# Start-up lookup of edges, PE's skip branches and the last norm in a four-layer graph network

## The reference

```python
# layer 0: out = segment_sum((x @ W)[src] * (edge_attr @ edge_w), dst) + b
# layer 1: agg = segment_sum(x[src], dst) / max(in_degree, 1); out = agg @ W_l.T + b_l + x @ W_r.T
# layer 2: out = segment_sum(x[src] * rsqrt(out_deg)[src] * rsqrt(in_deg)[dst], dst) @ weight + bias
# layer 3:
z = jnp.tanh(segment_sum((x @ gcn_w)[src] * norm[:, None], dst) + gcn_b)
g = jax.nn.sigmoid(z @ gate_w + gate_b)
out = jax.nn.relu((1.0 - g) * (x @ lin_w + lin_b) + g * z)
out = (out - out.mean(axis=0)) * jax.lax.rsqrt(out.var(axis=0) + 1e-5) * bn_gamma + bn_beta
```

## Time and profile before

| | |
|---|---|
| median of 3 runs | 2859.34 us (2858.33 to 2863.21) |
| profiled execution | 2858.09 us, span 2856.3 us, 35302 instructions |
| busy share of the span | PE 78%, POOL 58%, DVE 55%, ACT 18% |
| mean granted PE clock | 0.788 of 2.4 GHz |
| chain that ended last, by engine | PE 50%, POOL 17%, DMA 15%, issue 9%, DVE 7% |

### The profile page before, as it was taken

How to read it: one execution, slowest core, us unless ns; L and a number is a source line. 1 busy time by engine, 2 the same in 40 slices (tenths; PEclk the granted TensorE clock), 3 DMA queues, 4 the chain that set the end, 5 groups by cost and what they waited for, 6 DMA issues and landing times.

```text
span 2856.3 us, 35302 instructions
## 1 busy us (share of the span) xinstructions
PE 2239.6 (78%) x13018; PEld 1444.1 (51%) x13018; DVE 1570.8 (55%) x2582; ACT 500.8 (18%) x805; POOL 1664.6 (58%) x1781
## 2 busy tenths in 40 slices
PE   3678676777777787767778777878787999999991
PEld 2455554555554555545555555555554444455551
DVE  3566666666666666666666666666637111212117
ACT  1011111111111111111112111111114111111113
POOL 7777777777777777777777777777722000012220
PEclk7565767656777777777787888778888999999995
DMA  6233343434444444454554555555589687786641
GB/s 220 76 99 105 100 114 99 124 105 129 114 129 114 135 121 136 129 139 132 146 145 134 152 145 158 158 156 171 148 178 294 250 299 274 257 289 249 249 175 45
DMA packets 453788, 456.48 MB, mean 160 GB/s; under 512 B 160549, under 2 KB 399626, under 8 KB 453354
## 3 DMA queue, kind: packets, MB, share of 16 engines
q1 hardware_dynamic: 233694, 281.21, 29.2%
q0 software_dynamic: 53584, 109.44, 14.4%
q10 hardware_dynamic: 166332, 63.48, 9.1%
HBM read 368.88 MB, written 85.11 MB: 159 GB/s over the span
## 4 chain that ended last, share of the span: by engine, by line
PE 50%; POOL 17%; DMA 15%; issue 9%; DVE 7%; DVEq 1%; ACT 0%; POOLq 0%; SPq 0%; ACTq 0%
POOL big L714 17%; PE pb L1390 14%; DMA big<-xw,big 13%; PE pb L1493 9%; PE pb L1494 9%; PE pb L1311 8%; DVE big L903 4%; PE pb L1363 3%; PE pb L1353 2%; PE pb L1422 2%; PE pb L1369 1%; DMA big<-at 1%; PE pb L1511 1%; DVEq L838 1%; DMA xw<-big 1%
## 5 line engine op out<-in xcount | busy, mean ns | idle before, releaser
L714 POOL DMA_INDIRECT big<-xw,big x1612 | 1525.0, 946 | 493.5 <-issue 451.8
L1311 PE MATMUL pb<-big 64*128 64x512 f32 x808 | 322.2, 885 | 475.0 <-DVE big L903 473.2
L1390 PEld LDWEIGHTS pb<-big 128*128 128x128 f32 x3232 | 554.8, 267 | 227.5 <-issue 179.2
L903 DVE TENSOR_TENSOR big<-pb,big 128x512 f32<-128x512 f32 x404 | 260.3, 686 | 704.6 <-DMA big<-xw,big 695.0
L1597 ACT CAST tmp<-pb 128x784 f16<-128x784 f32 x392 | 318.3, 812 | 1646.3 <-PE pb L1363 1594.6
L1390 PE MATMUL pb<-big 128*128 128x64 f32 x3232 | 588.2, 358 | 0.4 <-DVE big L903 0.4
L829 DVE TENSOR_TENSOR big<-pb,big 128x2048 f16<-128x2048 f32 x196 | 447.7, 2284 | 0.8
L831 DVE TENSOR_TENSOR big<-pb,big 128x1568 f16<-128x1568 f32 x196 | 349.0, 1781 | 0.0
L1311 PEld LDWEIGHTS pb<-big 64*128 64x128 f32 x808 | 80.6, 244 | 506.0 <-DVE big L903 500.0
L1363 PE MATMUL pb<-big 128*128 128x98 f16 x3136 | 257.7, 238 | 37.1 <-DVE big L831 35.6
L1363 PEld LDWEIGHTS pb<-big 128*128 128x128 f16 x3136 | 237.6, 122 | 79.9 <-DVE big L831 45.9
(11 more groups left out here) (225 smaller groups left out, 1645.5 us busy)
## 6 DMA issues: line engine op xcount, KB each, us to landing
at<-tmp SPq DMA_DIRECT2D x196, 392.0 KB
big<-at SPq DMA_DIRECT2D x24, 3200.0 KB, 11.3
big<-at SPq DMA_DIRECT2D x24, 3072.0 KB, 19.7
big<-at ACTq DMA_DIRECT2D x32, 896.0 KB
big<-xw,big POOLq DMA_INDIRECT x1612
big<-in_ea SPq DMA_DIRECT2D x202, 64.0 KB
big<-at SPq DMA_DIRECT2D x13, 896.0 KB
big<-at ACTq DMA_DIRECT2D x24, 336.0 KB
```

Source lines behind the costliest of these rows:

```text
L714: nc.gpsimd.indirect_dma_start(gath[:, T8 * (n % NG) + t % T8, :], None, xw_d, bass.IndirectOffsetOnAxis(ap=src_i[:, t:t + 1], axis=0)).th ...
L903: nc.vector.tensor_tensor(msg[:, T8 * (n % 2) + 4 * q:T8 * (n % 2) + 4 * q + 4, :], PB[:, q, :].rearrange("p (t f) -> p t f", f=D), gath[: ...
L1311: last = nc.tensor.matmul(PB[:, q, :], ea[4 * ED * q:4 * ED * q + 4 * ED, n % NG, :], edge_w[4 * ED * q:4 * ED * q + 4 * ED, 4 * q:4 * q + ...
L1390: last = nc.tensor.matmul(PB[:, 2 + n % 2, 0:WIN], msg[:, T8 * (n % 2) + t, :], hot_win[:, T8 * (n % 2) + t, :], start=(t == 0), stop=(t = ...
```

## The change

1. **Lookup.** The 25 pairs of a lane are now neighbours (pair_dst is numbered by lane). So one coarse count per lane and one indirect DMA of 256 fine samples (FW) per lane serve all 25; DVE makes 25 counts over these 255 samples. The result, run_edge, has the wrong layout for the slot fetches; SP stores it to DRAM and reads it back turned (3200 single numbers). The slot fetch of batch 0 moves behind the gathers of step 0.
2. **x W.** The first weight matrix has a load of its own, x comes in four parts (turn 0; 1 and 2; 3 and 4; 5 and 6), the other weights after it. x W has four buffers. ACT waits for all stores before it loads x.
3. **Branches.** PE's bodies for k = 0, 1 and 2 and the one written out stand in one branch; the wait for layer 1's rows is in it, and the fast path waits for layer 1's sums (s_acc) alone. Call 3 keeps a branch of its own.
4. **Last norm.** PE adds y and the shift row in PSUM by two products with the identity matrix (y passes of the first three turns ahead of PE's sums, the rest after), six banks in rotation; DVE adds that to x times k_row. ACT scales the rows of turn t - 1 after the root of turn t, and the last turn's rows are scaled by DVE.

```diff
-Q_GROUPS = [0, 1, 5, 10, 15, 20]
-EARLY = 5
+FW = 256
-XT_CUT = NT // 2 + 1
+XT_CUTS = [0, 1, 3, 5, NT]
...
 @block.sync
-            sp.dma_start(wts[:, :, :], w_d[0:7].rearrange("w k n -> k w n")).then_inc(s_in["w"], 16)
+            sp.dma_start(wts[:, W_L0, :], w_d[W_L0]).then_inc(s_in["w0"], 16)
+            for part_of in range(4):
+                c0, c1 = XT_CUTS[part_of] * BT * P, XT_CUTS[part_of + 1] * BT * P
+                sp.dma_start(xT[:, c0:c1], xT_d[:, c0:c1]).then_inc(s_in[f"xT{part_of}"], 16)
+            sp.dma_start(wts[:, 1:7, :], w_d[1:7].rearrange("w k n -> k w n")).then_inc(s_in["w"], 16)
...
             for t in range(NT):
                 sp.wait_ge(s_rowev, 2 * t + 2)
                 sp.dma_start(xw_d[t * BT * P:(t + 1) * BT * P, :].rearrange("(b p) f -> p b f", p=P),
-                             xwS[:, T8 * (t % 2):T8 * (t % 2) + BT, :]).then_inc(s_rowst[t % 2], 16)
+                             xwS[:, T8 * (t % 4):T8 * (t % 4) + BT, :]).then_inc(s_rowst[t % 4], 16)
+                if t == NT - 2:
+                    sp.wait_ge(s_first, 2)
+                    sp.dma_start(first_d.rearrange("(p b) o -> p (b o)", b=NPB), run_edge[:, :]).then_inc(s_run, 16)
+            sp.wait_ge(s_run, 16)
+            with nc.allow_non_contiguous_dma(reason="3200 numbers, once"):
+                sp.dma_start(first_edge[:, :], first_d.rearrange("(b p) o -> p (b o)", p=P)).then_inc(s_firstin, 16)
             sp.dma_start(next_i, next_d).then_inc(s_in["rows"], 16)
...
 @block.gpsimd
-            for b in range(NPB):
-                if b in Q_GROUPS:
-                    pool.wait_ge(s_q, Q_GROUPS.index(b) + 1)
+            pool.wait_ge(s_q, 1)
+            pool.sem_inc(s_seen, 1)
+            nc.gpsimd.indirect_dma_start(first16_i, None, first16_d, bass.IndirectOffsetOnAxis(ap=first_q_i[:, 0:1], axis=0)).then_inc(s_f16, 16)
+
+            def slots_in(b):
+                if b == 0:
+                    pool.wait_ge(s_firstin, 16)
                     pool.sem_inc(s_seen, 1)
-                nc.gpsimd.indirect_dma_start(first16_i[:, b, :], None, first16_d,
-                                             bass.IndirectOffsetOnAxis(ap=first_q[:, b:b + 1], axis=0)).then_inc(s_f16[int(b >= EARLY)], 16)
...
+                if n == 0:
+                    slots_in(0)
                 if n % BL == BL // 2 and n // BL + 1 < NPB:
                     slots_in(n // BL + 1)
...
 @block.vector
+            nc.vector.tensor_scalar(less[:, 0:QN - 1], firstq_f[:, 1:QN], pair_dst[:, 0:1], None, ALU.is_lt, ALU.add, accum_out=before_q[:, 0:1]).then_inc(s_cut, 1)
...
             for b in range(NPB):
...
+                nc.vector.tensor_scalar(less[:, b % 4 * QN:b % 4 * QN + FW - 1], first16_f[:, 1:FW], pair_dst[:, b:b + 1], None, ALU.is_lt, ALU.add, accum_out=before_16[:, b:b + 1]).then_inc(s_cut, 1)
+            v.wait_ge(s_cut, 1 + NPB)
+            nc.vector.tensor_scalar(run_edge[:, :], before_16[:, :], first_q[:, 0:1], float(2 * FE), ALU.add, ALU.mult).then_inc(s_first, 1)
...
             for t in range(NT + 2):
                 if t < NT:
-                    nc.vector.tensor_tensor(blocks(x, t), blocks(x, t), wide(k_row), ALU.mult)
-                    scaled_at.append(bn_at(nc.vector.tensor_tensor(blocks(y, t), blocks(y, t), wide(b_row), ALU.add)))
+                    scaled = bn_at(nc.vector.tensor_tensor(blocks(x, t), blocks(x, t), wide(k_row), ALU.mult))
...
                 if t < NT:
-                    v.wait_ge(s_bn, scaled_at[t])
-                    sum_at.append(bn_at(nc.vector.tensor_tensor(blocks(x, t), blocks(x, t), blocks(y, t), ALU.add)))
+                    v.wait_ge(s_bn, scaled)
+                    v.wait_ge(s_bn_y, t + 1)
+                    for q, (b0, b1) in enumerate(((0, 4), (4, BT))):
+                        here = x[:, t * BT + b0:t * BT + b1, :]
+                        last = nc.vector.tensor_tensor(here, here, PB[:, 2 + 2 * (t % 3) + q, 0:(b1 - b0) * D].rearrange("p (b f) -> p b f", f=D), ALU.add)
+                    last.then_inc(s_bn_sum, 1)
...
+            v.wait_ge(s_bn, shift_at[NT - 1])
+            v.wait_ge(s_walk[4]["st0"], 16 * (NT // 2))
+            for b in range(NB - BT, NB):
+                last = nc.vector.tensor_scalar(xn[0][:, b - (NB - BT), :], x[:, b, :], rstd[:, b:b + 1], shift[:, b:b + 1], ALU.mult, ALU.add)
+            last.then_inc(s_walk[4]["xn0"], 1)
...
 @block.tensor
             g_off = off(pe)
-            general_pe(pe, 0, g_off)
-
             with pe.If(g_off > 0):
+                pe.wait_ge(s_y, NCH)
+                general_pe(pe, 0)
                 for t in range(NT):
...
-            general_pe(pe, 1, g_off)
-            pe.wait_ge(s_y, NCH)
+                general_pe(pe, 1)
+                general_pe(pe, 2)
+            pe.wait_ge(s_acc, NCK)
...
-            general_pe(pe, 2, g_off)
...
+            def y_rows(t):
+                for q, (b0, b1) in enumerate(((0, 4), (4, BT))):
+                    nc.tensor.matmul(PB[:, 2 + 2 * (t % 3) + q, 0:(b1 - b0) * D], ident[:, :], y[:, t * BT + b0:t * BT + b1, :], start=True, stop=False)
+
+            pe.wait_ge(s_gated["zts"], NCH)
+            pe.wait_ge(S["y"], 2 * NCH)
+            pe.wait_ge(s_gated["gb"], NCH)
+            for t in range(3):
+                y_rows(t)
             pe.wait_ge(s_bn, 6)
...
+            def shift_row(t):
+                pe.wait_ge(s_bn, 16)
+                for q, (b0, b1) in enumerate(((0, 4), (4, BT))):
+                    last = nc.tensor.matmul(PB[:, 2 + 2 * (t % 3) + q, 0:(b1 - b0) * D], ident[:, :], bn_row[:, 1, :].unsqueeze(1).broadcast_to([P, b1 - b0, D]), start=False, stop=True)
+                last.then_inc(s_bn_y, 1)
+
+            for t in range(3):
+                shift_row(t)
+            for t in range(3, NT):
+                pe.wait_ge(s_bn_sum, t - 2)
+                y_rows(t)
+                shift_row(t)
...
 @block.scalar
-                    if t >= 2 and q == 0:
...
+                    if t >= 4 and q == 0:
...
+            for h in range(4):
+                act.wait_ge(s_rowst[h], 16 * ((NT + 3 - h) // 4))
             act.wait_ge(s_const, 2)
...
-                act.wait_ge(s_bn, shift_at[t])
-                rows(4, t, t % 2, t // 2)
+                if t > 0:
+                    act.wait_ge(s_bn, shift_at[t - 1])
+                    rows(4, t - 1, (t - 1) % 2, (t - 1) // 2)
```

More of the change, by code:

```diff
@@ L270, in build @@
         cols = PB[:, 7, 0:P + KW]
[L272 removed]
+        s_in = {n: sem("in_" + n) for n in ("w0", "w", "edge_w", "xT0", "xT1", "xT2", "xT3", "vecs", "src", "edges", "firsts", "rows", "x")}
         s_const = sem("consts_made")
         s_rowxw, s_rowev = sem("xw_mm"), sem("xw_evac")
[L275 removed]
+        s_rowst = [sem(f"xw_stored{h}") for h in range(4)]
         s_tab = sem("dve_table_step")
         s_q = sem("coarse_counts")
[L278 removed]
+        s_f16 = sem("fine_firsts_in")
+        s_run, s_firstin = sem("run_edges_stored"), sem("first_edges_in")
         s_first = sem("first_edges_step")
@@ new lines, in general_pe @@
+            if k == 3:
+                for q in range(NCH):
+                    pe.wait_ge(s_w3["lo"], q + 1)
+                    if q >= 2:
+                        pe.wait_ge(s_redo["dve"], REDO_WALK + 3 * NT + q - 1)
+                    for b in range(CB * q, min(CB * q + CB, NB)):
+                        for part_of in range(2):
+                            last = nc.tensor.matmul(PB[:, 2 + q % 2, (b - CB * q) * P:(b - CB * q + 1) * P], parts_of[3][part_of][:, b, :], ident16[:, :], start=(part_of == 0), stop=(part_of == 1))
+                    last.then_inc(s_redo["pe"], 1)
+                pe.wait_ge(s_redo["dve"], REDO_WALK + 3 * NT + NCH)
@@ new lines, in general_pe @@
+            with pe.Fori(0, NH) as n:
+                if k == 0:
+                    pe.wait_ge(g["in"], before * NH * loads(k) + n * loads(k) + loads(k))
+                    for q in range(2):
+                        last = nc.tensor.matmul(PB[:, q, :], ea[:, 0, :], edge_w[:, 4 * q:4 * q + 4, :], start=True, stop=True)
+                    last.then_inc(g["ew"], 1)
+                    pe.wait_ge(g["msg"], 2 * n + 2)
+                else:
+                    pe.wait_ge(g[f"gathered{k}"], n * (16 * T8) + 16 * T8)
+                pe.sem_inc(s_seen, 1)
+                with pe.Fori(0, NB) as b:
+                    pe.wait_ge(g["hot"], before * NH * NB + n * NB + b + 1)
+                    pe.wait_ge(g["sum"], before * NH * NB + n * NB + b)
+                    for t in range(T8):
+                        ends = {"start": t == 0, "stop": t == T8 - 1}
+                        if k == 0:
+                            last = nc.tensor.matmul(PB[:, 2, 0:D], g_hot[0][:, t, :], msg[:, t, :], **ends)
+                        else:
+                            nc.tensor.matmul(PB[:, 2, 0:P], g_rows[k][:, t, 0:D], g_hot[k][:, t, :], start=(t == 0), stop=False)
```

(19 more changed lines are left out.)

119 lines of the change are left out of this document (30 added, 89 removed).

## The result

The changed kernel takes 2833.41 us (median of 4 runs, 2831.54 to 2835.22), the kernel before 2860.62 beside it (2858.33 to 2863.21): a ratio of 0.9904, interval 0.989 to 0.9918, 27.2 us less. The profiled execution took 2831.54 (span 2829.7) where that of before took 2858.09: 26.55 us less. The forecast was 2835.6 for the median and 23.7 us of gain.

The account below looks back on a forecast made before the run. POOL's issue count was taken to bound stage one, with separate chains at start-up, before layer 2 and in the last norm. Gains 11.8 + 6.3 + 5.6 = 23.7 us gave 2834.4 profiled, 2835.6 as median; range 2825 to 2848.

Parts of the forecast that it names:

- Start-up: Before stage one: x W stored and first edges looked up sooner, first gather at 33.2 instead of 46.21; 11.8 us gained, bounds 8 and 14.
- rival (b): Start of stage one: POOL waits for the first edges, or the stores land late; 3 to 8 us lost, 2841; chance 0.14.
- Branch: PE ahead of layer 2's first product: one merged branch of 6.0 us remains, product starts 6.3 us earlier; bounds 0 and 12.
- (c): PE's branch ahead of layer 2: one long jump pays both fetches, so the branch part gains nothing; 2841.9; chance 0.08.
- (d): PE's branch ahead of layer 2: the merged branch is quick, 5.7 us more gained, 2830; chance 0.07.
- Last norm: Kernel's end: DVE's turn falls from 4.96 to 4.05 us and last rows finish sooner; 5.6 us gained, bounds 6.5 and -0.6.
- Rival (a): Last norm: PE stays at 1.2 GHz, 6.2 us a turn, DVE waits 6.2 us in all; 2841.8; chance 0.14.
- The claim underneath: Stage one: POOL hardly ever waits for data; 1636 issues of 1.25 us make 2045.6 us, so delaying its first gather delays everything.

## Why the prediction was right

The three chains added as said; the sum was 2.9 us short (23.7 against 26.55), inside its own bounds, by these terms and -0.4 in between, at the end of layer 1.

**Start-up, 11.8 forecast, 13.5 come.** The last store landed at 30.6, not 32.5, and the first gather stood at 31.43, not 33.2. Inside that two guesses were off and nearly cancelled: SP's first store went out at 16.69, not 13.9 (the load of the window table to all partitions held SP 4.38 us, where in the kernel before it had held it 0.68; the DMA engines were full at that point, 1.00 from 4 to 8 us, where they had stood at 0.84), and the first landing, 22.5, was sooner than 23.4. The order of SP's DMAs was counted, a longer issue was not. That the two errors cancelled is luck. So is a third thing: DVE's copy and table were priced against the gathered rows alone, not against POOL's issues; they ended at 28.7, 2.7 us ahead of the first gather, and nothing was lost. The 1.25 us of the slot fetch came back exactly. The first edges were ready far ahead of the 42 at which they are wanted: their read landed at 33.9, where I had 40 (36.5 to 44) from the earlier trace rows and some us for x. Both ends of that range are real, but as two cases, not as a spread: 3.6 to 4.6 us where the read goes out over 1.2 us ahead of x's load, 10 to 20 where with it or behind. The changed kernel is on the good side by 1.24 us, so rival (b) was nearer than the result shows. "DMA: Bandwidth & Descriptors" of the Trainium skill (its line of 512 bytes) made it likelier; the trace agrees with it on the store of the degrees (13.3 us for 6400 small numbers, DMA full at 17 GB/s); this read, of 12.5 KB, still landed in 4.5 us, too soon to matter.

**Branch, 6.3 forecast, 6.1 come,** and 1.0 more behind it: I had the clock low for five us of products again, and it was back at 1.00 after 3.3 (by 2188.9). Rivals (c) and (d) both fail on the one branch line of 6.2. "Advanced Engine Details and Errata" of the Trainium skill (Control Flow Timing) gives a compare-and-branch about 108 ns: the trace agrees where the branch falls through (0.10 and 0.06 us) and not where it jumps over a body (6.2). "Runtime: NRT & Kernel Launch" of the Trainium skill (Instruction fetch mechanics) says that a taken branch to code outside the fetched window waits for a fetch; that fits, but not by length alone: of two jumps over bodies of one length, those of parts 1 and 2, one took 0.22 and the other 5.58, and the jump over part 3, the longest of the four, 0.34. Which jumps pay was not settled, and no view here shows a fetch.

**Last norm, 5.6 forecast, 6.3 come.** The turn is 4.02 (4.05 forecast), DVE's first wait 2.39 (2.3), the first aggregate 0.5 late as said. The last rows brought 1.3, not 1.5, since DVE's seven scalings take 0.27 each, not 0.21. What I had not seen is the 0.8 ahead of the turns: the y passes end just as the sums are due, so those run at the full clock. Rival (a), PE at 1.2 GHz throughout, is wrong: the clock was back some 5 us into the shift passes, and the row of 2794 to 2796 has it at 1.00.

**The claim underneath,** that stage one is a count of POOL's issues, holds on the two traces I compared (2045.6 and 2046.9 us from first to last gather) and not in general: the degree store goes with a wait of POOL of 0 to 5.5 us, and on two chips POOL waits for PE all through the stage.

## What to carry to other kernels

Where two chains end together, price them as one: here one alone was worth 2.6 us, the other nothing, both 14.8. Where the ordinary path jumps over a body that never runs, look at what the jump takes, and put the body behind the program (here 12.9 to 6.8 us by merging, to 0.7 by moving). Before work is reordered in a start-up, look at the DMA share: at 1.0, only bytes taken out of it counted. Ask then which engine waits for a load that is put off, and what its work will meet: here DVE's copy met POOL's first gathers, and that took back the gain. A small read on the critical path belongs well ahead of a large load: 1.2 us ahead it landed in 4.5 us, 0.02 us ahead in 10.5.

## What the runs showed of the hardware

On two chips the kernel before takes 3333 to 3339 us instead of 2857 to 2861. The traces of the other kernels there have nearly all of that in stage one: outside it they are 1 to 11 us longer than the same edits would make them on the other chips. In the kernel with the old last norm PE waits 551 us for ACT's copies of the adjacency, where in the changed kernel's trace the same products wait 28.5 us, for DVE. ACT in turn waits for something that the trace calls remote; by the order of the code it can be the landing of those copies' stores. That longest wait of PE (us in total, times, longest):

```profile
PE pb L1366 <- ACT tmp L1603: 551.2, 149, 12.0
```

Whether those stores land later there, and why, was not tried.

The issue of an indirect DMA on POOL, 0.94 us nearly everywhere, is long while DVE is in one of a few steps on wide tiles in SBUF. Under the copy of 6336 columns it takes 3.85 to 4.02 us (five traces), under the table of 1616 columns 1.45 to 1.73; in each of these pairs the issue ends within 0.9 us behind DVE's step. The 2.28 and 2.29 us at 132.65 and 111.32 in the changed kernel also fall on such steps of DVE, of 1616 columns (1.83 us). In the nine traces where the copy met no issue of POOL, no issue in the start was slow. No kernel moved DVE's copy alone, so this rests on the times agreeing, not on an edit; giving the copy its bias early, with the other loads behind, was not tried.
